# One semaphore for each batch of eight gathers in the four gather passes of a graph network

## The reference

```
x = norm(x + segment_sum(x[dst] * dis[src] * dis[dst], src))            # layer 0, summed by src
x = norm(x + segment_sum((x @ W[r])[rel, src], dst))                    # layer 1, summed by dst
e = silu(silu([x[src], x[dst], w] @ W1 + b1) @ W2 + b2)                 # layer 2: an MLP on each edge
x = norm(x + mlp([x, segment_sum(e, src)]))
h = relu(gcn(x)); x = norm(x + gcn(h) + x @ We + be)                    # layer 3: gcn twice, by dst
# gcn(x) = segment_sum((x @ W)[src] * dinv[src] * dinv[dst], dst) + b, with a self edge at each node
# src is drawn evenly over the nodes; dst = int(50000 * u**2), so low nodes are drawn more often
```

## Time and profile before

| What | us |
|---|---|
| median of 3 runs | 5162.78 |
| lowest and highest of them | 5155.84, 5186.35 |
| span of the profiled execution | 6462.1 |
| its passes e0, e1, e3, e4 | 685, 652, 660, 661 |
| its gathers of the edge MLP with the steps beside them | 690 |
| the rest of it | 3114 |

### The profile page before, as it was taken

How to read it: one execution, slowest core, us unless ns; L and a number is a source line. 1 busy time by engine, 2 the same in 40 slices (tenths; PEclk the granted TensorE clock), 3 DMA queues, 4 the chain that set the end, 5 groups by cost and what they waited for, 6 DMA issues and landing times. The chain is left out here.

```text
span 6462.1 us, 74448 instructions
## 1 busy us (share of the span) xinstructions
PE 3919.6 (61%) x19983; PEld 3086.7 (48%) x19983; DVE 2177.2 (34%) x4653; ACT 1422.3 (22%) x3080; POOL 2886.1 (45%) x2799
## 2 busy tenths in 40 slices
PE   3333451668656742667466759888952669626697
PEld 2122121667422322666265646776732668426586
DVE  7444790324645620124311102343530112102134
ACT  0000000001333420112200126443420223302135
POOL 2555406663566766661555540000146660366602
PEclk8555575555666765555555569999975555755569
DMA  3000131111445641223734436554631222412235
GB/s 99 2 2 2 47 113 33 43 42 42 155 175 202 234 153 38 66 70 138 264 99 101 107 116 202 181 180 181 227 113 35 69 69 84 145 36 69 69 106 177
DMA packets 354959, 692.13 MB, mean 107 GB/s; under 512 B 183337, under 2 KB 185254, under 8 KB 339130
## 3 DMA queue, kind: packets, MB, share of 16 engines
q1 hardware_dynamic: 148381, 491.73, 21.7%
q10 hardware_dynamic: 118428, 130.12, 6.0%
q0 software_dynamic: 87808, 66.01, 5.8%
HBM read 350.87 MB, written 349.58 MB: 108 GB/s over the span
## 5 line engine op out<-in xcount | busy, mean ns | idle before, releaser
L1058 PE MATMUL e_ring<-e_msgs,e_hot 128*128 x6272 | 1419.4, 413 | 1091.3 <-issue 1082.7
L1058 PEld LDWEIGHTS e_ring<-e_msgs,e_hot 128*128 128x128 f32 x6272 | 1385.0, 328 | 1127.4 <-issue 1125.9
L925 POOL DMA_INDIRECT e_msgs<-y,index_D x784 | 741.4, 946 | 640.9 <-POOLq L77 261.1
L977 DVE TENSOR_TENSOR e_hot<-e_nodes,keys_D 128x2048 f32<-128x2048 f32 x147 | 336.9, 2292 | 1596.9 <-remote 872.0
L599 POOL DMA_INDIRECT list_D<-d_place,d_target x392 | 456.2, 1164 | 326.6 <-DVEq L553 210.5
L925 POOL DMA_INDIRECT e_msgs<-y,index_S x392 | 396.8, 1012 | 387.7 <-DVE index_S L963 198.3
L599 POOL DMA_INDIRECT list_S<-s_place,s_target x392 | 390.6, 996 | 362.8 <-DVEq L553 247.5
L1241 POOL DMA_INDIRECT m_far<-x,index_S x392 | 390.9, 997 | 347.9 <-DMA pairs_by_edge<-m_far 221.4
L1410 PE MATMUL m_ring<-m_region,m_hot 128*128 x1568 | 375.9, 426 | 215.7 <-issue 213.3
L925 POOL DMA_INDIRECT e_msgs<-x_by_relation,index_D x392 | 374.0, 954 | 210.4 <-issue 112.8
L1410 PEld LDWEIGHTS m_ring<-m_region,m_hot 128*128 128x128 f32 x1568 | 348.1, 328 | 244.3 <-issue 242.2
(11 more groups left out here) (368 smaller groups left out, 5846.1 us busy)
## 6 DMA issues: line engine op xcount, KB each, us to landing
x_by_relation<-d_stage SPq DMA_DIRECT2D x98, 1024.0 KB
agg<-e_stage ACTq DMA_DIRECT2D x196, 256.0 KB
n_in<-agg SPq DMA_DIRECT2D x42, 896.0 KB, 5.6
x<-n_out SPq DMA_DIRECT2D x28, 896.0 KB, 3.6
m_keyrow<-keys_by_step SPq DMA_DIRECT2D x49, 512.0 KB
m_region<-pairs_by_edge SPq DMA_DIRECT2D x49, 512.0 KB
messages<-m_region SPq DMA_DIRECT2D x98, 256.0 KB
m_region<-messages SPq DMA_DIRECT2D x49, 512.0 KB, 4.1
```

Of the source, the lines that this page charges most:

```text
L925: pool.indirect_dma_start(out=msgs[:, (i % HELD) * D:(i % HELD + 1) * D], out_offset=None, in_=source, in_offset=bass.IndirectOffsetOnAxis ...
L977: nc.vector.tensor_tensor(hot[g % 2][:, :, :], bc(nodes[:, 0:P].unsqueeze(1), [P, GS, P]), bc(order["keys"][:, g * GS:(g + 1) * GS].unsque ...
L1058: mm = nc.tensor.matmul(ring[:, bass.ds(bucket, D)], hot[g % 2][:, k, :], msgs[:, bass.ds(tile, D)], start=False, stop=False, skip_group_c ...
```

## The change

Two semaphores take the place of the eight in the gather passes. All eight gathers of batch b signal number b % 2, so a batch adds 128 to it. POOL waits at the first gather of batch b for batch b - 2 to have landed in full, and never inside a batch. SP waits once a batch for the full count of it and raises `s_ready` by 8. The waits for room, what DVE, PE and ACT do, and all the data moved stay as they are.

```diff
-        s_land = K["slots_dma"]
-        before = K["landed"]()
+        s_batch = K["batch_dma"]
+        passed = next(K["stairs"])
+        before = [16 * SLOTS * ((BATCHES + 1 - r) // 2) * passed for r in range(2)]
...
             for i in range(T):
+                b = i // SLOTS
                 if i >= HELD and i % SLOTS == 0:
                     pool.wait_ge(s_room, (i - HELD) // SLOTS + 1)
-                if i >= SLOTS:
-                    pool.wait_ge(s_land[i % SLOTS], before + 16 * (i // SLOTS))
+                if i % SLOTS == 0 and b >= 2:
+                    pool.wait_ge(s_batch[b % 2], before[b % 2] + 16 * SLOTS * (b // 2))
                 pool.indirect_dma_start(
...
-                ).then_inc(s_land[i % SLOTS], 16)
+                    in_offset=bass.IndirectOffsetOnAxis(ap=order["index"][column][:, i:i + 1], axis=0)).then_inc(s_batch[b % 2], 16)
...
-                for i in range(b * SLOTS, (b + 1) * SLOTS):
-                    sp.wait_ge(s_land[i % SLOTS], before + 16 * (i // SLOTS + 1))
-                    sp.sem_inc(s_ready, 1)
+                sp.wait_ge(s_batch[b % 2], before[b % 2] + 16 * SLOTS * (b // 2 + 1))
+                sp.sem_inc(s_ready, SLOTS)
```

More of the change, by code:

```diff
@@ L920, in _ @@
             for i in range(T):
+                b = i // SLOTS
                 if i >= HELD and i % SLOTS == 0:
                     pool.wait_ge(s_room, (i - HELD) // SLOTS + 1)
-                if i >= SLOTS:
-                    pool.wait_ge(s_land[i % SLOTS], before + 16 * (i // SLOTS))
+                if i % SLOTS == 0 and b >= 2:
+                    pool.wait_ge(s_batch[b % 2], before[b % 2] + 16 * SLOTS * (b // 2))
                 pool.indirect_dma_start(
                     out=msgs[:, (i % HELD) * D:(i % HELD + 1) * D], out_offset=None, in_=source,
-                    in_offset=bass.IndirectOffsetOnAxis(ap=order["index"][column][:, i:i + 1], axis=0)
-                ).then_inc(s_land[i % SLOTS], 16)
+                    in_offset=bass.IndirectOffsetOnAxis(ap=order["index"][column][:, i:i + 1], axis=0)).then_inc(s_batch[b % 2], 16)
         @block.sync
@@ L2325, in gnn @@
         K["slots_dma"] = [semaphore(f"slot{r}") for r in range(SLOTS)]
+        K["batch_dma"] = [semaphore(f"batch{r}") for r in range(2)]
+        K["stairs"] = itertools.count()
         passes = itertools.count()
```

## The result

The changed kernel is slower by 0.66%: 5209.99 us against 5176.69 us, medians of 20 runs each, ratio 1.0066 (95% interval 1.0043 to 1.0088). It came out 35 us over the forecast of 5175 us and 2 us over the upper end of the range. One run of e2 (14340.8 us) and one of e3 (5964.3 us) lay far outside all others and are left out of their ratios.

A forecast was written before the change was run, and what follows sets the result against it. The prediction took POOL's issue of gathers to bound the passes. To 5162.8 us it added 0 for POOL's waits, 0 for SP's relays and 12 for the coarser signal: 5175 us, range 5115 to 5208.

The forecast's parts named there:

- What bounds a pass: In the gather passes of the timed runs, POOL's issue of gathers sets the pace and PE waits for tiles.
- The slow stretches: PE and SP slowing together in the profile, a matmul every 2.80 us; read as the price of recording, not the kernel.
- that sum: Whole kernel: with 3114 us outside the gathers unchanged without recording, 2049 us remain for five gather phases, 410 us each.
- POOL's wait for room: POOL waiting for room from SP, 59.8 us in one profiled gather pass; claimed to stay after the change.
- POOL's waits at nothing: On POOL in the gather passes: removing 1348 waits for landed gathers gains 0, at most 23 us.
- SP's relays at nothing: On SP in the gather passes: 1568 relays become 196, 23 us off SP beside the gathers; price 0.
- The coarser signal at 12 us: Groups wait for whole batches; three passes have the last group 3.6 to 6.1 us late: 11 to 18 us, 12 taken.
- the late start: At the start of order-D passes, group 1 needs 10 tiles, gets them with 16, 7.6 us later; caught up.
- the gates alone: Tile counts that groups need to start, now met by whole batches; this term's upper size is 18 us.
- The real stretches: Rival: PE's and SP's slow stretches occur in timed runs too, and fewer relays return 296 us: 4867 us; chance 0.06.
- the costly waits: Rival: POOL's removed waits do cost time, gaining 23 us (5140 us) up to 81 us (5082 us); chance 0.12.
- A PE that is always behind: Rival: PE sets the pass end in timed runs too, 14 us lost in three passes, +41 us, 5204 us; chance 0.12.

The follow-up runs named there:

- e2: SP's half of the change alone against the kernel before: eight semaphores, POOL unchanged, SP raises the count by 8 once a batch; ratio 1.0016.
- e3: POOL's half alone against the kernel before: sixteen semaphores, POOL waits once a batch for batch b - 2, SP relays every tile; ratio 0.9987.
- e5: The changed kernel, but every gather of a batch carries the batch's wait; ratio 1.0034.
- e4: The changed kernel measured and recorded once more, no edit; ratio 1.0038.
- e12: Against e2, the last two batches are relayed tile by tile; ratio 0.9993.
- e6: Against e3, still sixteen semaphores, but POOL waits once a batch on a count that SP raises when a batch has landed; ratio 0.9991.
- e1: As a run: the kernel before, recorded and timed once more, no edit; ratio 1.0005. Elsewhere the same name means a gather pass.
- e8: The changed kernel with the batch's wait at every fourth gather; ratio 1.0049.
- e13: Against the changed kernel, the two semaphores alternate every four gathers, and POOL waits every four gathers for the four lying eight back; ratio 1.0054.
- e14: The changed kernel with two semaphores whose numbers lie eight apart; ratio 1.0057.
- e15: The changed kernel, but POOL waits on a count that SP raises once a batch; ratio 1.0065.
- e16: Against the changed kernel, one semaphore for all gathers, and POOL waits at each batch for batch b - 1; ratio 1.092.

## Why the prediction was wrong

**What bounds a pass: right.** The slow stretches were a matter of one recording, and in all the later ones POOL's issue sets the pace, at 1.25 to 1.26 us a gather. I had put the true pitch between 0.95 and 1.26 us, since the passes seemed to have some 410 us each; they take 500 to 524 us. The error was in the other part of that sum: the stages outside the passes were stretched in that recording as well, above all the first one (955 us up to the first gather, later 666). POOL's wait for room, which I took to stay, belonged to that recording too. A slip of reading changes nothing here: my last run of matmuls of e1 was cut by the window that I asked for. It is 506 matmuls from 2898.01 to 3006.01, so that pass was 657 us long, not 652.

**POOL's waits at nothing: right.** Run e5 against run e4 shows it: a satisfied wait on nearly every gather leaves the pitch at 1.249 us. The Trainium skill (Advanced Engine Details and Errata, Network/Comms) has 50 to 100 ns for a sequencer that reads a semaphore; whatever that read costs, none of it shows in POOL's pitch.

**SP's relays at nothing: right.** They took 17 ns before and after.

**Where the sum started.** It started from 5162.8 us, the median of 3 runs; 20 runs gave 5176.7. So 14 of the 35 us over the forecast are not of the change, and 21 are: it cost 33 us where I had 12.

**The coarser signal at 12 us: right in mechanism, some two thirds too large.** It measured 2.1 to 2.6 us in each of three passes, 7.2 us, where I had worked out 3.6 to 6.1 a pass. The last batch is ready 11.15 us after PE starts its last three groups (7.17 us to the last gather and 3.98 from there), not 10.1, so less of the two groups' 13.7 us is in excess. Its place is shown by e12, and the late start is caught up as forecast.

**The step that failed** is in the part on POOL's waits: "Up to 16 gathers may be in flight instead of 8, but the wait for a landing was 0.6 us in all." I weighed the waits and the number of gathers in flight, both of which are free (runs e3, e6), and gave no price at all to what the diff names first, that all gathers signal two semaphores instead of eight. The trace of before has no row for it, and the bound should have been drawn from both sides; instead the upper end of the sum, +18 us, held the gates alone. It costs some 1.8 us at a stop in every 112 gathers, 22 us of the 33.

**The rivals.** None was right. The real stretches fell with run e1, the costly waits with e5. A PE that is always behind would have given a similar loss, but PE idles about 3 us before each group, and e12 shows the late start to be harmless: its 5204 us resembled the result, its mechanism did not.

**The profile after.** The relays, the pitch of 1.26 us, more matmuls in the first 156 us of e1 (478 instead of 96) and timed runs that did not shorten came as forecast. The span fell by 1252 us instead of 100 to 500, and the change had no part in it: the kernel before, recorded again, fell by as much.

**What stays open** is why. The gaps were there in the six kernels with two semaphores (the changed one, e5, e8, e13, e14, e15) and in e16 with one, and in none of the nine with three, four, eight or sixteen. They come after 113 gathers of a pass and then every 112 (every 113 with one semaphore), whatever the waits, turns and numbers. What ends them is known, a landing and 1.80 us; what makes POOL ask for that landing, and what it does in the 1.80 us, the trace does not show. Nor does it show why three semaphores are enough. There the gather in the same place starts 2.5 us after the one two places ahead of it, as every other does, so POOL does not wait for that landing.

## What to carry to other kernels

Waits of POOL's gathers that were already satisfied cost nothing here, so to thin them out gained nothing; look first whether anything ever stood in such a wait. To make a signal coarser cost something only at the end of a pass, where the last tiles come, and a fine signal for the last two batches took that back. Where many gathers share completion semaphores, try three or more rather than one or two, and compare the pitch of the gathers over the whole pass, not over its first sixteen.

## What the runs showed of the hardware that I had not expected

- With one or two completion semaphores for all gathers of a pass, POOL stopped after 113 gathers, and again every 112 (every 113 with one), until a recent gather had landed and 1.80 to 1.82 us more; with three, four, eight or sixteen, never. With two semaphores the extra is about 1.8 us over its usual 0.30 us. The Trainium skill (DMA: Bandwidth & Descriptors, Why a DMA increments its semaphore by 16 and not by 1) asks for a semaphore for each slot in flight, because a count can be filled by another transfer. No run here tests that. In these kernels a batch starts only when the one before it on the same semaphore has landed in full, so its count cannot be filled by another; for the time, three semaphores for eight gathers each gave 1.0005.
- A single recording was 1299 us longer than the timed runs. In a stretch of its e1, PE started a matmul every 2.80 us and a relay of SP took 0.69 us, while POOL still gathered at 1.26 us. The seventeen later recordings, among them one of the same kernel, had none of it. A span far above the timed runs is a reason to distrust who waits for whom in it.
